# The second bank of two paired products is emptied by the vector engine instead of the scalar engine

## What is computed

```
h = tok(x, W)                                  # patches, real DFT, projection to 64
h = h + attn0(layernorm(h))                    # 8 heads of width 8, with relative bias
h = h + ffn0(layernorm(h))                     # first: relu(x @ Wi.T + bi), 64 -> 128
                                               # then two routed layers 128 -> 128, then 128 -> 64
h = h + attn1(layernorm(h))                    # 8 heads of width 8, no bias
h = h + ffn1(layernorm(h))                     # top 2 of 8 experts

attn: q, k, v = split(x @ qkv_w.T + qkv_b)     # scale 8 ** -0.5 on q
      softmax(q @ k.T * scale + bias) @ v, then the projection
```

## Time and profile before

| | |
|---|---|
| median of 3 runs | 4034.71 us (4033.22 to 4037.4) |
| profiled execution, its own time | 4041.78 us |
| its span | 4040.0 us |
| PE busy | 3811.9 us, 94% |
| DVE busy | 2886.2 us, 71% |
| ACT busy | 2619.9 us, 65% |
| POOL busy | 860.0 us, 21% |
| mean granted TensorE clock | 0.981 of full |

### The profile page before, as it was taken

How to read it: one execution, slowest core, us unless ns; L and a number is a source line. 1 busy time by engine, 2 the same in 40 slices (tenths; PEclk the granted TensorE clock), 3 DMA queues, 4 the chain that set the end, 5 groups by cost and what they waited for, 6 DMA issues and landing times.

```text
span 4040.0 us, 62363 instructions
## 1 busy us (share of the span) xinstructions
PE 3811.9 (94%) x21508; PEld 1330.2 (33%) x21508; DVE 2886.2 (71%) x4955; ACT 2619.9 (65%) x4768; POOL 860.0 (21%) x1263
## 2 busy tenths in 40 slices
PE   6988999999999999999999999999999999999896
PEld 3223333333333333333333333333333333333232
DVE  3866767778686777867678676777867677777672
ACT  0555767667676666767667676666767667676564
POOL 4122113122121322213122121312213122121211
PEclk7899999999999999999999999999999999999998
DMA  5203211222012122111222122122111222111100
GB/s 106 40 15 60 43 36 33 46 48 44 22 35 56 33 43 43 37 34 33 46 48 43 27 38 49 32 43 47 38 29 33 50 44 43 31 36 25 28 6 6
DMA packets 119067, 156.36 MB, mean 39 GB/s; under 512 B 24847, under 2 KB 66575, under 8 KB 118717
## 3 DMA queue, kind: packets, MB, share of 16 engines
q1 hardware_dynamic: 118753, 152.38, 19.0%
HBM read 120.01 MB, written 29.36 MB: 37 GB/s over the span
## 4 chain that ended last, share of the span: by engine, by line
PE 81%; ACT 8%; issue 4%; DVE 3%; SPq 2%; DMA 1%; POOL 1%; ACTq 0%; POOLq 0%; DVEq 0%
PE acc L911 23%; PE side_st L897 21%; PE nat L885 19%; PE side_st L854 3%; PE side_st L750 3%; PE side_st L727 2%; ACT prob L1101 2%; PE side_st L840 2%; ACT hidden L1073 2%; PE side_st L807 1%; DVE tile_max L1294 1%; ACT hidden L1019 1%; PE side_st L772 1%; SPq L525 1%; PE side_st L765 1%
## 5 line engine op out<-in xcount | busy, mean ns | idle before, releaser
L1294 DVE TENSOR_REDUCE tile_max<-nat 128x1 f32<-128x512 f32 x4096 | 2585.7, 684 | 1002.6 <-PE nat L885 972.0
L1101 ACT ACTIVATE prob<-side_st 128x512 f32<-128x512 f32 x4096 | 2205.8, 600 | 1271.7 <-PE side_st L897 1236.8
L897 PE MATMUL side_st<-q_rows,k_rows 99*128 99x512 bf16 x4096 | 1562.6, 384 | 45.9 <-ACT prob L1101 28.9
L885 PE MATMUL nat<-k_rows,q_rows 96*128 96x512 bf16 x4096 | 1532.2, 385 | 30.2 <-DVE tile_max L1294 24.0
L911 PE MATMUL acc<-prob,v_padded 128*32 128x512 f32 x8192 | 1096.1, 607 | 14.5 <-ACT prob L1101 13.5
L897 PEld LDWEIGHTS side_st<-q_rows,k_rows 99*128 99x128 bf16 x4096 | 398.6, 98 | 1213.9 <-ACT prob L1101 812.1
L885 PEld LDWEIGHTS nat<-k_rows,q_rows 96*128 96x128 bf16 x4096 | 400.8, 98 | 508.4 <-DVE tile_max L1294 276.1
L1455 POOL TENSOR_SCALAR max_parts<-neg_max 128x16 bf16<-128x16 f32 x128 | 26.5, 207 | 1868.4 <-DVE neg_max L1301 1868.3
L911 PEld LDWEIGHTS acc<-prob,v_padded 128*32 128x32 f32 x8192 | 162.3, 108 | 377.4 <-ACT prob L1101 216.0
L840 PE MATMUL side_st<-ln_rows,w 64*128 64x512 f32 x512 | 139.5, 622 | 28.7 <-ACT hidden L1073 23.2
L1380 POOL TENSOR_SCALAR ln_s<-ln_s 128x8 f32<-128x8 f32 x64 | 13.0, 203 | 676.8 <-DVE ln_s L1202 673.2
(11 more groups left out here) (124 smaller groups left out, 1994.5 us busy)
## 6 DMA issues: line engine op xcount, KB each, us to landing
q_rows<-q_scratch SPq DMA_DIRECT2D x576, 64.0 KB
k_rows<-k_scratch SPq DMA_DIRECT2D x192, 192.0 KB
x_rows<-in_x SPq DMA_DIRECT2D x62, 512.0 KB, 6.3
q_scratch<-hidden SPq DMA_DIRECT2D x32, 384.0 KB
k_scratch<-hidden SPq DMA_DIRECT2D x96, 128.0 KB
group_weights<-in_routed SPq DMA_DIRECT2D x64, 129.0 KB, 2.1
q_rows<-max_rows SPq DMA_DIRECT2D x512, 3.0 KB
out_h<-out_rows SPq DMA_DIRECT2D x16, 256.0 KB, 2.1
```

The source lines that it names most:

```text
L885: eng.matmul(NAT[use % len(NAT)][:, :], QA[u][0:K_NAT, h, c:c + P], KA[u][0:K_NAT, h, kh * 512:kh * 512 + 512], start=True, stop=True)\
L897: eng.matmul(RING[TILE_BANK[n0 + n]][:, :], KA[u][0:K_ALL, h, t * P:t * P + P], QA[u][0:K_ALL, h, half * 512:half * 512 + 512], start=True ...
L1101: eng.activation(prob[:, n % TILES, :], RING[TILE_BANK[n0 + n]][:, :], ACT.Exp).then_inc(exp_done, 1)
L1294: eng.tensor_reduce(mx[:, q % 2, j // 8, j % 8 // 2, j % 2:j % 2 + 1], NAT[use % len(NAT)][:, :], AX.X, ALU.max).then_inc(nat_free, 1)
```

## The change

For QK and H1 the loop over both banks on ACT becomes one activation for bank 0. DVE gets a piece in both stages: one `tensor_scalar` for bank 1, with multiply and add for QK, with add and maximum with 0 for H1. In H1 the waits for both writes and the counts of `hid_ready` and `xt_used` move to DVE. The waits that guard the destination (`split_p` and `y_ready` for QK, `y_ready` for H1) are made on both engines. Line numbers behind the change shift: DVE's QK piece is line 1207, its H1 piece line 1213, `reduce_tile` line 1307, ACT's exponential line 1095, its H1 line 1031.

```
--- before.py
+++ after.py
@@ -1014,11 +1014,10 @@
                     eng.wait_ge(y_ready, at(n["FY8"]))
                     if n["QK"] == 0:
                         eng.wait_ge(s_dve, SET_DVE)
-                    for par in range(2):
-                        bk = full(n, par)
-                        eng.activation(by_parity(QF, par), bk[:, :].rearrange("p (j q) -> p j q", j=4),
-                                       ACT.Identity, bias=bqk[more[0]][:, 0:1], scale=scl[:, 0:1])\
-                            .then_inc(side_free[par], 1)
+                    bk = full(n, 0)
+                    eng.activation(by_parity(QF, 0), bk[:, :].rearrange("p (j q) -> p j q", j=4),
+                                   ACT.Identity, bias=bqk[more[0]][:, 0:1], scale=scl[:, 0:1])\
+                        .then_inc(side_free[0], 1)
                 elif name == "OTR":
                     eng.wait_ge(hres, at(n["OTR"]))
                     eng.wait_ge(y_ready, at(n["FY8"]))
@@ -1028,15 +1027,10 @@
                     eng.sem_inc(ot_ready, 1)
                 elif name == "H1":
                     eng.wait_ge(y_ready, at(n["FY8"]))
-                    for par in range(2):
-                        bk = full(n, par)
-                        eng.activation(HE[:, 0, :].rearrange("p (g j a q) -> p a j g q", g=G, j=4, a=2)[:, par],
-                                       bk[:, :].rearrange("p (j g q) -> p j g q", j=4, g=G), ACT.Relu,
-                                       bias=bi[:, 0:1]).then_inc(side_free[par], 1)
-                    for par in range(2):
-                        eng.wait_ge(side_free[par], at(n[f"bank{par}"] + 1))
-                        eng.sem_inc(hid_ready, 1)
-                    eng.sem_inc(xt_used, 1)
+                    bk = full(n, 0)
+                    eng.activation(HE[:, 0, :].rearrange("p (g j a q) -> p a j g q", g=G, j=4, a=2)[:, 0],
+                                   bk[:, :].rearrange("p (j g q) -> p j g q", j=4, g=G), ACT.Relu,
+                                   bias=bi[:, 0:1]).then_inc(side_free[0], 1)
                 elif name in ("L0", "L1"):
                     ll = int(name[1])
                     if ll == 0:
@@ -1174,6 +1168,9 @@
             def nat4(bk, cols):
                 return bk[:, 0:4 * cols].rearrange("p (j c) -> p j c", j=4)
 
+            def by_parity(tile, par):
+                return tile.rearrange("p (j a q) -> p a j q", j=4, a=2)[:, par]
+
             def passed_both(n):
                 for par in range(2):
                     eng.wait_ge(side_free[par], at(n[f"bank{par}"] + 1))
@@ -1203,6 +1200,22 @@
                 elif name == "LN2":
                     eng.wait_ge(ln_p, at(6 * n["LN2"] + 3))
                     eng.tensor_reduce(ln_s[:, 2, :], sq[:, :, :], AX.X, ALU.add).then_inc(ln_d, 1)
+                elif name == "QK":
+                    eng.wait_ge(split_p, at(4 * n["QK"]))
+                    eng.wait_ge(y_ready, at(n["FY8"]))
+                    bk = full(n, 1)
+                    eng.tensor_scalar(by_parity(QF, 1), bk[:, :].rearrange("p (j q) -> p j q", j=4),
+                                      scl[:, 0:1], bqk[more[0]][:, 0:1], ALU.mult, ALU.add)\
+                        .then_inc(side_free[1], 1)
+                elif name == "H1":
+                    eng.wait_ge(y_ready, at(n["FY8"]))
+                    bk = full(n, 1)
+                    eng.tensor_scalar(HE[:, 0, :].rearrange("p (g j a q) -> p a j g q", g=G, j=4, a=2)[:, 1],
+                                      bk[:, :].rearrange("p (j g q) -> p j g q", j=4, g=G),
+                                      bi[:, 0:1], 0.0, ALU.add, ALU.max).then_inc(side_free[1], 1)
+                    passed_both(n)
+                    eng.sem_inc(hid_ready, 2)
+                    eng.sem_inc(xt_used, 1)
                 elif name == "QV":
                     eng.wait_ge(vc_done, at(n["QV"]))
                     for par in range(2):
```

## The result

| | before | with the change |
|---|---|---|
| median of the runs | 4036.06 us (4033.22 to 4037.81, 4 runs) | 4010.27 us (4003.90 to 4011.17, 4 runs) |
| ratio | | 0.9932, 95% interval 0.9919 to 0.9945 |
| profiled execution, its own time | 4041.78 us | 4011.17 us |
| its span | 4040.0 us | 4009.4 us |

The change saves 25.8 us by the medians; 27.4 were forecast.

A forecast was written before the change was run, and what follows sets the result against it. PE was taken to bound the kernel, with some 47 us of its waits as the pool. 14 x (0.50 + 0.87 + 0.43) = 25.2, with 1.7 and 0.5, made 27.4 us: 4034.7 - 27.4 = 4007.3 us, range 4001 to 4021.

The forecast's parts named there:

- Place A: QK at slot 127, pairs 0 to 13: the exponential behind ACT's single piece starts earlier and PE's wait goes, 0.50 us.
- Place B: H1 at slot 166, pairs 0 to 13: exponential and scores product come 0.87 us earlier; 0.36 us of wait stays.
- Place C: QK at slot 210, QV at 213, pairs 0 to 13: with DVE's piece at 0.68 us, QV starts 0.43 us earlier.
- the rival of a slow piece: DVE's piece takes 1.05 us, so Place C and the like lose 0.37 us each; 4013 us, chance 0.06.
- The rule of the Trainium skill: PSUM access overhead is about 125 ns for DVE, 51 for ScalarE; implied a 0.85 us piece, 0.26 us at Place C.
- DVE's cover: Reductions delayed behind DVE's new pieces cost PE nothing at all three places; 0.9 us to spare at Place B, the thinnest.
- The irregular places: Three QV waits (serial start, pairs 0 and 14) gain 1.7 us; L0 after H1 in two shortened middles gains 0.5 us.
- a `nat` product waits for DVE in these slots: Sign that the prediction is wrong: PE's `nat` product waits for a DVE reduction in the touched slots.
- the half taken back: Rival: PE arrives earlier at a DMA landing or POOL's chains and half the saving is lost; 4021 us, chance 0.08.
- no effect: Rival: DVE gets to bank 1 no earlier than ACT did and the wait changes hands; 4035 us, chance 0.06.
- DVE as what PE waits for: Rival: DVE's pieces delay reductions, the ring of three `nat` banks runs dry, 33.6 us lost; 4068 us, chance 0.04.
- The clock: Rival: a stretch at 1.2 instead of 2.4 GHz, 2.0 us in pair 5, more or less blurs any case.

The follow-up runs named there:

- operands run: Changed kernel with the scale left out of DVE's QK piece and the bias out of its H1 piece (computes something else); 4009.99 us, one run.
- the runs with two and three added reductions: Changed kernel with two or three extra reductions of the same bank into a spare column ahead of DVE's H1 piece; 4019.35 and 4030.31 us.
- the second profile of the kernel before: Kernel before the change, run again unedited for one more profile; 4032.45 us, one run.
- H1 alone: Changed kernel with QK put back on ACT, so only H1 is split over ACT and DVE; 4022.61 us, 0.9965 of the kernel before.
- the control: Changed kernel run again unedited; 4010.86 us, 0.9937 of the kernel before.
- QK alone: Changed kernel with H1 put back on ACT, so only QK is split over ACT and DVE; 4021.68 us, 0.9964 of the kernel before.

## Why the prediction was right

**What bounds the kernel.** Right: PE's waits in the touched slots were the pool. They fell by 17.6 us before scores and 5.8 before QV, 23.4 in all, and the time by 25.8. A pair was to take 239.1 us and takes 239.2.

**Place A**, forecast 0.50: 0.50, gone as said. **Place B**, 0.87: 0.88, with 0.36 left from the same releaser, as said. **Place C**, 0.43: 0.30. The step that was off is the price of DVE's piece. It was taken from the copy of 682 ns; it is 802, and 0.12 us of the 0.13 lies there. Within the stated bounds (0.60 to 1.05) I chose by engine, size and source, and gave the operands, which stood in ACT's row (776 against 600), only the 0.06 of the rival of a slow piece. The operands run shows the cause: without per-partition operands the piece is the 681 ns of a copy, so the 0.12 us are theirs.

The rule of the Trainium skill that was weighed (Perfetto Trace Analysis, section Optimizing Scalar/DVE Operations) was set aside for a wrong reason: ACT's 776 ns, a piece with two operands, was held against DVE's 682 ns, a copy without any. Like against like, ACT copies such a bank in 592 ns:

```profile
L1009 ACT ACTIVATE ln_rows<-side_st 128x512 f32<-128x512 f32 x64 | 37.9, 592 | 24.9 <-PE side_st L765 24.9
```

So DVE is the dearer engine for this data, as in the rule: by 90 ns for a copy, by 55 to 60 for the H1 piece (741 against 681 to 686) and by 26 to 30 for the QK piece (802 against 772 to 776). The estimate of 0.85 us that I took from the rule was nearer to 0.80 than my 0.68, but by luck: the same section says that profiled lengths hold about twice the overhead, and with twice the 74 ns the estimate would have been 0.92.

**DVE's cover.** Forecast 0.9 us to spare at B; 0.72 were there, and the runs with two and three added reductions both point back to that figure. "I cost all three at nothing" was right, and at B it was right by little more than one reduction (0.60).

**The irregular places.** Forecast 1.7 for three QV waits. The QV waits fell by 5.8, of which 14 x 0.31 = 4.3 are place C, so 1.5. One by one, the serial start's wait went from 1.71 to 1.13, pair 0's 0.69 is gone, and pair 14's went from 1.47 to 1.16. The two shortened H1 I gave 0.5, and that was too much: L0's wait for `hid_ready` in pair 14 went from 1.28 to 1.10, and pair 0 has no such wait in either profile, so 0.2.

"For QK in the first phase I count nothing" missed a loss. Slots 5 to 24 of the first phase take 15.48 us in the second profile of the kernel before and in that of H1 alone, and 16.58 in the control and in six other kernels with QK moved, 1.1 us more (the other four profiles hold some lower clock in these slots). Here the sign "a `nat` product waits for DVE in these slots" did come up, with the 0.52 us at slot 13.

**The sum.** 14 x (0.50 + 0.88 + 0.30) = 23.5, plus 1.5 and 0.2, less 1.1: 24.1 us, against 25.8 and 25.9 by medians. The rival of a slow piece was true in a small part; the half taken back and no effect did not come. DVE as what PE waits for came in the first phase alone; in the steady pairs the 0.72 us of slack kept it away.

**The clock.** The prediction took a stretch at the lower clock for blur. In the steady pairs it is not: there it comes only behind QV of slot 213. The one in pair 5 of the first profile of the kernel before, granted clock near the end of the row:

```profile
1659.10:1662.50 3.40, 3.40 (x14) 0.84 (x7) 1.70 (x4) 1.41 (x3) 3.02 (x3) 0.50 0.00 0
```

It begins behind the QV that had waited 1.03 us. In the three profiles in which ACT empties both banks of QK, 6 of the 42 stretches from slot 209 to 215 in pairs 0 to 13 hold such a fall to half the clock and take 1.1 to 1.3 us longer. In the ten profiles with QK moved, where QV waits 0.72 us or less, none of 140 does. So the change has a second gain that the sum does not hold. What sets it is not shown; an estimate from these counts is two stretches per execution, 2.4 us, which with the 24.1 makes 26.5.

Outside the steady pairs a stretch costs more than the 2.0 us of the prediction. Pair 0, in windows of the run with QK alone and of the run with three added reductions (length, busy by engine, granted clock near the end):

```profile
214.30:466.50 252.20, 231.90 (x1281) 81.65 (x1280) 183.32 (x308) 156.58 (x297) 61.90 (x87) 0.97 0.18 37
```

```profile
214.00:481.00 267.00, 240.99 (x1282) 84.94 (x1281) 188.35 (x316) 155.25 (x295) 61.90 (x87) 0.92 0.18 35
```

Its length is 252.2 us at a mean clock of 0.97 and 267.0 at 0.92, while pair 2 of the same runs differs by 0.2. Of the 14.8 us some 2, by an estimate, are the added reductions. The other runs gave 256 to 264 for it. Such stretches at 1.2 GHz come after the serial start, in the shortened middles and near slot 95 of pair 0, behind or within longer waits of PE (3.14 us at slot 4 and 8.23 us at slot 96 of pair 0 in the first profile), and what sets them is open. They hold a large part of the several us by which single executions of this kernel scatter, so the verdicts above rest on the stretches of steady pairs and on medians.

## What to carry to other kernels

Where one engine bounds the kernel and runs an order fixed by hand, read one period of its time line and redo it by hand with the changed starts: here it gave each place to 0.01 us wherever the durations were right. Do the same for the places outside the period; the one that was left out lost 1.1 us. Moving work to the engine with 71% load cost nothing here until its delay passed the slack of the ring behind it, and then it cost in full; so compute the slack in the slot, not from the load. When one piece must wait behind another on its engine and another engine waits for it, look at its place in the order too: doing QK and QV before the reduction brought 17 us, for no work moved at all, where the move to another engine had brought 26. And hold like against like: a price taken from a row without the operands was 0.12 us short.

## What the runs showed of the hardware

Each per-partition operand of DVE's `tensor_scalar` on a 128x512 float32 bank cost 60 ns (802, 741 to 743 and 681 ns for two, one and none), on top of what a plain copy takes. On ACT a QK piece with scale and bias operands took 772 to 776 ns and an H1 piece with bias 681 to 686, against 592 for a copy of that size (the earlier trace rows have 600 for an exponential). Two pieces on two engines, out of two banks filled by one pair of products, ran side by side without getting longer: ACT's QK piece took 772 ns beside DVE's and 776 before, and DVE's QK piece 802 ns beside ACT's and 810 where it ran ahead of it; DVE's H1 piece took 741 ns beside ACT's and 741 with both banks on DVE.
